# An MoE decoder layer: the first expert matrix of each slot loaded from HBM instead of copied from a resident set

## The reference

```python
logits = jnp.einsum('bsd,ed->bse', x, router_w)
probs = jax.nn.softmax(logits, axis=-1)
topk_vals, topk_idx = jax.lax.top_k(probs, K)          # K = 2 of E = 8
for eid in range(e):
    w = jnp.sum(jnp.where(idx == eid, vals, jnp.zeros((), x.dtype)), axis=-1)
    h = jax.nn.gelu(x_flat @ w1[eid].T, approximate=False)   # w1: (8, 1024, 256)
    y = h @ w2[eid].T                                        # w2: (8, 256, 1024)
    out = out + w[:, None] * y
```

## Time and profile before

| | |
|---|---|
| median of 3 runs | 930.38 us (927.92 to 937.87) |
| the profiled execution's span | 939.3 us |
| PE busy | 711.5 us (76%) |
| DVE busy | 377.1 us (40%) |
| ACT busy | 326.8 us (35%) |
| POOL busy | 215.8 us (23%) |
| mean granted TensorE clock | 0.880 of full speed |
| `hidden` matmuls (L1592) | 148.2 us, 1248 of them |
| `expert_out` matmuls (L1603) | 144.3 us, 624 of them |
| copies to `w1c` | ACT 41.1 us (39 of 1056 ns), DVE 27.2 us (39 of 698 ns) |
| moved by DMA | 71.08 MB |

### The profile page before, as it was taken

How to read it: one execution, slowest core, us unless ns; L and a number is a source line. 1 busy time by engine, 2 the same in 40 slices (tenths; PEclk the granted TensorE clock), 3 DMA queues, 4 the chain that set the end, 5 groups by cost and what they waited for, 6 DMA issues and landing times.

```text
span 939.3 us, 13839 instructions
## 1 busy us (share of the span) xinstructions
PE 711.5 (76%) x4099; PEld 452.6 (48%) x4100; DVE 377.1 (40%) x790; ACT 326.8 (35%) x541; POOL 215.8 (23%) x265
## 2 busy tenths in 40 slices
PE   7473239999999876647888722898899898998980
PEld 3232102222222355422226622887788787887870
DVE  2153237888886366635327850111111111111113
ACT  3121226667767533323542110323222322223212
POOL 1021100111111112121110573222332233223332
PEclk9786678999999997857769955999999999999995
DMA  6999990000003407688238343111111111111105
GB/s 210 121 167 166 167 113 2 2 1 1 1 1 122 96 2 135 101 120 141 95 131 272 91 121 121 19 26 29 31 23 23 28 28 30 22 28 29 21 10 179
DMA packets 67342, 71.08 MB, mean 76 GB/s; under 512 B 14548, under 2 KB 60141, under 8 KB 67310
## 3 DMA queue, kind: packets, MB, share of 16 engines
q1 hardware_dynamic: 54574, 58.03, 31.7%
q0 software_dynamic: 8512, 8.44, 5.6%
q10 hardware_dynamic: 4224, 4.19, 1.6%
HBM read 50.45 MB, written 21.40 MB: 76 GB/s over the span
## 4 chain that ended last, share of the span: by engine, by line
PE 39%; DMA 30%; issue 8%; DVE 8%; SPq 6%; POOL 5%; ACT 2%; POOLq 1%; DVEq 0%; ACTq 0%
DMA acc<-yw,mt 12%; PE ps L1313 7%; DMA scrq<-parts 7%; PE ps L1322 6%; DMA mt<-metas 5%; PE ps L1258 5%; PE ps L1603 4%; PE ps L1592 4%; SPq L397 3%; DMA qst<-mT 3%; PE ps L1406 2%; POOL metas L665 2%; PE ps L1479 2%; POOL xt L694 2%; PE ps L1472 2%
## 5 line engine op out<-in xcount | busy, mean ns | idle before, releaser
L903 DVE TENSOR_REDUCE nmx<-ps 128x1 f32<-128x512 f32 x256 | 160.4, 683 | 55.7 <-PE ps L1258 55.7
L750 ACT ACTIVATE probs<-ps 128x512 f32<-128x512 f32 x256 | 133.6, 608 | 94.5 <-PE ps L1313 94.4
L1603 PE MATMUL ps<-wexp,hidT 128*128 x624 | 144.3, 384 | 17.6 <-ACT hidT L856 12.3
L1592 PEld LDWEIGHTS ps<-xtT,w1c 128*128 128x128 f32 x1248 | 147.7, 195 | 4.3 <-DVE w1c L363 1.5
L1592 PE MATMUL ps<-xtT,w1c 128*128 128x128 f32 x1248 | 148.2, 278 | 1.8 <-ACT xtT L850 1.8
L1603 PEld LDWEIGHTS ps<-wexp,hidT 128*128 128x128 f32 x624 | 115.4, 190 | 39.7 <-issue 25.5
L1214 DVE TENSOR_SCALAR yw<-ps,mt 128x256 f32<-128x256 f32 x39 | 18.9, 484 | 259.2 <-PE ps L1603 259.2
L1313 PE MATMUL ps<-qst,kst 99*128 (+1 forms) x256 | 95.9, 394 | 35.4 <-DMA qst<-mT 33.4
L1258 PE MATMUL ps<-kst,qst 96*128 (+1 forms) x256 | 93.9, 393 | 33.7 <-DVE nmx L903 17.2
L856 ACT ACTIVATE hidT<-ps 128x1024 f32<-128x1024 f32 x39 | 39.9, 1024 | 221.1 <-PE ps L1592 221.1
L694 POOL DMA_INDIRECT xt<-x2d,mt x39 | 43.3, 1110 | 209.7 <-DVE yw L1214 150.4
(11 more groups left out here) (166 smaller groups left out, 696.6 us busy)
## 6 DMA issues: line engine op xcount, KB each, us to landing
wexp<-in_w1T SPq DMA_DIRECT2D x8, 1024.0 KB, 5.0
wexp<-in_w2T SPq DMA_DIRECT2D x8, 1024.0 KB, 8.4
qst<-scrq SPq DMA_DIRECT2D x24, 256.0 KB, 9.4
kst<-scrk SPq DMA_DIRECT2D x24, 256.0 KB, 19.8
qst<-scr_q SPq DMA_DIRECT2D x24, 256.0 KB, 8.5
scrq<-parts SPq DMA_DIRECT2D x4, 768.0 KB, 18.4
scrk<-parts SPq DMA_DIRECT2D x4, 768.0 KB, 18.9
scr_q<-parts SPq DMA_DIRECT2D x4, 768.0 KB, 3.4
```

Source lines behind the costliest of these rows:

```text
L750: act.activation(probs[n % 8][:, :], ps[:, 4 + n % 3, :], ACT.Exp).then_inc(s_exp, 1)
L903: dve.tensor_reduce(nmx[j % 2][:, k:k + 1], ps[:, slot, :], AX.X, ALU.max, negate=True).then_inc(s_mfree, 1)
L1592: mm = pe.matmul(ps[:, 2 * (j % 2) + f // 4, f % 4 * P:(f % 4 + 1) * P], w1c[j % 2][:, k * FF + f * P:k * FF + (f + 1) * P], xtT[j % 2][:, ...
L1603: mm = pe.matmul(ps[:, 4 + j % 2, 0:D], hidT[j % 2][:, f * P:(f + 1) * P], wexp[:, ds(e * EW + KD * FF + f * D, D)], start=(f == 0), stop= ...
```

## The change

- `wexp` holds only the second matrices (`EW` = 2048 numbers a partition in place of 4096). `load_expert` issues one 1 MB load in place of two. Expert 6 no longer waits for the attention's outcome, and expert 7 no longer for the first `load_meta`: all are loaded in one go after cross-attention. PE waits once, ahead of slot 0, for all of `wexp`.
- `copy_w1` and its calls on DVE and ACT are gone, with their reads of the plan and their waits.
- A new `load_w1(t)` on SP reads the slot's expert from the plan, waits from slot 2 on that `hidden(t-2)` has freed the buffer, and loads the 1 MB of the slot's first matrix from HBM into `w1c[t % 2]`. Slots 0 and 1 are issued as soon as the plan is there, ahead of the wait for the scattered `metas`. In the loop `load_w1(k+2)` stands ahead of the wait for scatter k and of `load_meta(k+4)`.
- `hidden` waits for one semaphore for each buffer, in place of one for each half.

```diff
-    EW = KD * FF + KF * D
+    EW = KF * D
...
-    def copy_w1(engine, copy, t, j, k):
-
-        e = engine.value_load(plan[0][0:1, ds(t, 1)], min_val=0, max_val=NE - 1)
-        engine.wait_ge(s_we, 32 * (e + 1))
-        if not (isinstance(t, int) and t < 2):
-            engine.wait_ge(s_mm1, t - 1)
-        copy(w1c[j % 2][:, k * FF:(k + 1) * FF], wexp[:, ds(e * EW + k * FF, FF)]).then_inc(s_w1c[k], 1)
-
...
+        def load_w1(t, j):
+            e = sp.value_load(plan[0][0:1, ds(t, 1)], min_val=0, max_val=NE - 1)
+            if not (isinstance(t, int) and t < 2):
+                sp.wait_ge(s_mm1, t - 1)
+            sp.dma_start(w1c[j % 2][:, :].rearrange("p (k f) -> p k f", k=KD),
+                         w1T[ds(e, 1)].rearrange("e (k p) f -> p (e k) f", p=P)).then_inc(s_w1c[j % 2], 16)
 
         sp.wait_ge(s_planned, 1)
+        for t in range(2):
+            load_w1(t, t)
...
-        load_expert(NE - 1)
         with sp.Fori(0, NSLOT // 4 - 1) as i:
             for j in range(4):
+                load_w1(4 * i + j + 2, j + 2)
                 sp.wait_ge(s_sc, 16 * (4 * i + j + 1))
                 load_meta(4 * i + j + 4, j)
...
-        def hidden(t, j):
-
-            for k in range(KD):
-                pe.wait_ge(s_w1c[k], t + 1)
+        def hidden(t, j, turn):
+
+            pe.wait_ge(s_w1c[j % 2], 16 * (turn + 1))
             pe.wait_ge(s_xtT, t + 1)
...
         pe.wait_ge(s_planned, 1)
+        pe.wait_ge(s_we, 16 * NE)
```

More of the change, by code:

```diff
@@ L283, in decoder_layer @@
     s_h = sem("gelu_ready")
-    s_w1c = [sem(f"w1_copied_{k}") for k in range(KD)]
+    s_w1c = [sem(f"w1_loaded_{k}") for k in range(2)]
     s_mm2 = sem("expert_out_ready")
@@ L459, in load_expert @@
             if e > 0:
[L460 to L463, removed]
+                sp.wait_ge(s_we, 16 * e)
+            sp.dma_start(wexp[:, ds(e * EW, KF * D)].rearrange("p (k n) -> p k n", k=KF),
                          w2T[ds(e, 1)].rearrange("e (k p) n -> p (e k) n", p=P)).then_inc(s_we, 16)
@@ L471, in _ @@
         sp.wait_ge(s_pv2, QT * NB)
-        for e in range(NB - 1, NE - 2):
+        for e in range(NB - 1, NE):
             load_expert(e)
@@ L476, in _ @@
         sp.wait_ge(s_x2[1], 16 * NB)
-        load_expert(NE - 2)
+        def load_w1(t, j):
[4 more added lines that the diff above has]
+                         w1T[ds(e, 1)].rearrange("e (k p) f -> p (e k) f", p=P)).then_inc(s_w1c[j % 2], 16)
         sp.wait_ge(s_planned, 1)
+        for t in range(2):
+            load_w1(t, t)
         for i in range(2):
@@ L489, in _ @@
             load_meta(t, t)
-        load_expert(NE - 1)
         with sp.Fori(0, NSLOT // 4 - 1) as i:
             for j in range(4):
+                load_w1(4 * i + j + 2, j + 2)
                 sp.wait_ge(s_sc, 16 * (4 * i + j + 1))
                 load_meta(4 * i + j + 4, j)
-        for t in range(NSLOT // 4 * 4, NSLOT):
-            sp.wait_ge(s_sc, 16 * (t - 3))
-            load_meta(t, t % 4)
+        for t in range(NSLOT // 4 * 4, NSLOT + 2):
+            if t - 2 < NSLOT:
+                load_w1(t - 2, t - 2)
+            if t < NSLOT:
+                sp.wait_ge(s_sc, 16 * (t - 3))
+                load_meta(t, t % 4)
         sp.wait_ge(s_sc, 16 * NSLOT)
@@ L856, in gelu @@
             act.activation(hidT[j % 2][:, :], bank(2 * (j % 2), 2), ACT.Gelu).then_inc(s_h, 1)
[L858 to L863, removed]
         copy_xtT(0, 0)
@@ L866, in _ @@
         copy_xtT(1, 1)
-        w1_half(2, 2)
         with act.Fori(0, NSLOT // 4) as i:
@@ L871, in _ @@
                 copy_xtT(4 * i + j + 2, j + 2)
-                w1_half(4 * i + j + 3, j + 3)
         for t in range(NSLOT // 4 * 4, NSLOT):
@@ L1204, in _ @@
         dve.tensor_copy(plan[1][:, :], planf[2][:, :]).then_inc(s_planned, 1)
-        def w1_half(t, j):
-            copy_w1(dve, dve.tensor_copy, t, j, 0)
         def weigh(t, j):
@@ L1214, in weigh @@
             dve.tensor_scalar(yw[j % 2][:, :], ps[:, 4 + j % 2, 0:D], mt[j % 4][:, 1:2], None, ALU.mult).then_inc(s_yw, 1)
-        dve.wait_ge(s_planned, 1)
-        w1_half(0, 0)
-        w1_half(1, 1)
         for t in range(4):
-            w1_half(t + 2, t)
             weigh(t, t)
@@ L1223, in _ @@
             for j in range(4):
-                w1_half(4 * i + j + 2, j)
                 weigh(4 * i + j, j)
         for t in range(NSLOT // 4 * 4, NSLOT):
-            if t + 2 < NSLOT:
-                w1_half(t + 2, t)
             weigh(t, t)
@@ L1603, in expert_out @@
                 mm = pe.matmul(ps[:, 4 + j % 2, 0:D], hidT[j % 2][:, f * P:(f + 1) * P],
-                               wexp[:, ds(e * EW + KD * FF + f * D, D)], start=(f == 0), stop=(f == KF - 1))
+                               wexp[:, ds(e * EW + f * D, D)], start=(f == 0), stop=(f == KF - 1))
             mm.then_inc(s_mm2, 1)
@@ L1609, in tile @@
             if not (last and t + 1 >= NSLOT):
-                hidden(t + 1, j + 1)
+                hidden(t + 1, j + 1, 2 * i + (j + 1) // 2)
             if not (last and t + 2 >= NSLOT):
@@ L1615, in _ @@
         pe.wait_ge(s_planned, 1)
+        pe.wait_ge(s_we, 16 * NE)
         turn_tile(0, 0, 0)
-        hidden(0, 0)
+        hidden(0, 0, 0)
         turn_tile(1, 1, 0)
```

## The result

The changed kernel takes 1023.5 us (median of 4 runs, 1020.4 to 1025.0) against 930.6 us for the kernel before: a ratio of 1.097, 95% interval 1.092 to 1.102, 93 us longer. The forecast was 1016 (965 to 1050). The profiled execution's span went from 939.3 to 1022.6 us.

A forecast was written before the change was run, and what follows sets the result against it. The kernel before was taken as bound by scatter, SP, `mt`, gather, scatter at 8.49 us a slot. A second, two-slot ring (+45 us) and the falling clock (+41) make +86 on 930.4: 1016 us, range 965 to 1050.

The forecast's parts named there:

- The bound before: Expert stage before: scatter, SP, load of `mt`, POOL's gather, next scatter bound each slot, 8.49 us; PE's own work 7.32 us.
- The removed copies at 0: Expert stage: the 39 copies on each of DVE and ACT lie in those engines' waits; removing them gains 0 us.
- The second ring: Expert stage: the load for slot k+3 waits behind scatter k on SP; 19.48 us per two slots, +45 us.
- `hidden` to `weigh`: Part of a two-slot turn from start of `hidden`, through the slot's turn and `expert_out`, to start of `weigh`: 7.52 us.
- `mt` to the load: Part of a two-slot turn: SP reads the plan again and issues `load_w1` after `mt`, 0.95 us.
- the load: Part of a two-slot turn: the 1 MB first matrix lands in 5.0 us; each microsecond more or less is 18 us in total.
- The clock: TensorE's clock in the expert stage falls in PE's idle gaps: 18 pairs of slots at 2.3 us, +41 us.
- The pairing: Expert stage: slots come in pairs, with 3.7 us of PE's idle time in one piece ahead of each odd slot.
- the old ring: Expert stage: scatter, SP, load of `mt`, gather, next scatter, 8.5 us a slot; limits how closely the even slot follows.
- the gathers and `mt` against the loads: Expert stage: the gather of slot k+4 meets the 1 MB load but has about 7 us to spare, counted 0.
- The stages ahead: Ahead of the expert stage: loading 8 MB less and issuing slots 0 and 1 at the plan changes 0 us, within 2.
- the forecast's own case: Whole kernel: load of 4.4 to 5.5 us, clock fall costing 1.5 to 3 us, spanning 995 to 1035 us; chance 0.68.

The follow-up runs named there:

- `before_mt8`: Kernel before with eight buffers of `mt` in place of four, so the load for slot k+8 waits for scatter k: 890.7 us, ratio 0.948.
- `nocopy`: Kernel before, with each copy to `w1c` from slot 2 on taking one column in place of 1024, waits kept: 927.8 us, ratio 0.995.
- `filler_all`: Changed kernel with 9 extra identity matmuls on PE ahead of every slot's `hidden`: 989.0 us, ratio 1.055.
- `early`: Changed kernel with SP issuing the matrix load of slot k+3 ahead of its wait for scatter k: 941.7 us, ratio 1.011.
- `half`: Changed kernel loading only the first 128 rows (0.5 MB) of the matrix from slot 2 on: 981.4 us, ratio 1.050.
- `actq`: Changed kernel with the matrix loads from slot 2 on issued by ACT on its own queue, behind its copy of `xtT`: 997.5 us, ratio 1.063.
- `filler`: Changed kernel with 13 extra identity matmuls on PE in every odd slot, ahead of its wait for the load: 998.5 us, ratio 1.071.
- `actq_mt8`: Changed kernel with matrix loads from slot 2 on issued by ACT on its own queue, and eight buffers of `mt`: 885.6 us, ratio 0.945.
- `noload`: Changed kernel without the matrix loads in the slots' loop, later slots reusing those of slots 0 and 1: 934.1 us, ratio 0.996.

## Why the prediction was right

- **The bound before** (ring scatter, SP, `mt`, gather, 8.5 us, and PE's 7.3 behind it): shown by `before_mt8`, 7.25 us a slot, 890.7 us for a forecast of 885 to 895.
- **The removed copies at 0:** 1.4 us of the stage in `nocopy`, within the 2 us that I had allowed. Its median is 5 us lower, and where the rest of that comes from is not shown.
- **The second ring, 45 us:** 50.8 us with the clock's part taken out by `filler_all`, a turn of 19.8 for 19.48. The terms, in the turn shown above: `hidden` to `weigh` 10.51 for 7.52, of which 2.97 is the low clock (6.70 - 3.73), `weigh` to the scatter 1.36 for 1.30, scatter landing 3.70 for 3.8, to the issue of `mt` 0.82 for 0.81, `mt` to the load 1.17 for 0.95, the load 4.79 for 5.0, landing to PE 0.23 for 0.1. The mean turn is 0.3 us longer than the sum, 5 us in 17 turns. SP's step from `mt` to the load, taken from a row of four small loads, is the term that was most under-sized, by 0.22. `early` shows the cause: where the load stands, not that it is there.
- **The clock, 41 us:** 39.0 us of the stage, 40.3 us in the busy time of `hidden`. The one compares two kernels, the other two groups of instructions, and they agree. The pairing was there from slot 3 on, with waits of about 5 us where I had 3.7: I had let the even slot follow after the old ring's 8.5 us, but with the odd slot late the old ring is early, and the even slot follows after PE's own 7.3 (plus the time lost to the clock). That the term came out so close is in part luck: it took for granted that a gap of 3.7 us drops the clock every time, and in `half` waits of about that length did so 8 times of 12, with 171.1 - 148.2 = 22.9 us lost in `hidden`. The gaps of the changed kernel were longer, and there it fell each time.
- **What was too simple:** the gathers and `mt` against the loads. I counted 0 for the changed kernel, and that holds since nothing of theirs is on the second ring. It does not hold for the cures. In `actq` about 63 us come from `mt` landing late on the old ring; in `early` 4 of the 9 us are late landings of `mt`, and the rest is open. My expectation for both left this out.
- **The stages ahead, 0:** right as far as it can be told. The profiled execution before was itself one with a low clock in cross-attention, which fits that it lay 1% above its median.
- **A slip in the numbers:** the span of 995 to 1035 for the forecast's own case does not follow from the bounds named beside it; a load of 4.4 us with a fall of 1.5 gives 991, one of 5.5 with a fall of 3 gives 1038.

The Trainium skill's page "TensorE: Matmul & The Clock Gate", section "HAM oscillation — how this bites in real kernels", describes the loop that idles for a DMA and restarts at half rate each time. The changed kernel's trace agrees, with 5.25 to 6.70 us in place of 3.73 for `hidden` behind each of the 18 waits of about 5 us; behind the shorter waits of `half` and `filler` it was so in some slots and not in others. The Trainium skill's page "DMA: Bandwidth & Descriptors", section "Anatomy of one DMA — SWDGE (gpsimd) path", gave an estimate of 4.4 us for the load; the trace has 4.9 as the median.

## What to carry to other kernels

A transfer that an in-order queue issues inherits every wait that stands ahead of it: before adding one, write down what the queue waits for at that place and close the ring from there to the consumer and back; one line moved ahead of one wait was worth 82 us here. If the new wait lets TensorE idle for several us a turn, price the clock as well, here 39 us beside 51 for the ring. And a busy engine at 90% is no sign that it is the bound: the chain of waits of a queue that moved 1 KB a slot was, and four more small buffers gave 5%.

## What was not expected of the hardware

- A 1 KB load landed in 3.6 us (`actq`) and 3.8 us (`actq_mt8`) as the median, in place of 1.7, when ACT's queue had a 1 MB load under way, issued about 1.5 us before it. In `actq` this made each slot 1.8 us longer.
- More work made the kernel faster: 9 extra products of the identity in every slot took 34 us off the median (1023.5 to 989.0).
- In `filler` waits of 2.41 and 2.52 us ended in a lower clock, and others of 2.23 and 2.55 us did not; in `half` one of 3.71 did and one of 3.52 did not.
- The stages ahead of the expert stage, the same in `early` and `noload`, took 568.9 us in one and 585.8 us in the other, and over all twelve executions they were by and large longer where cross-attention was granted a lower clock (581.9 us and more below 0.70, 575.8 and less above 0.80).
